# A decoder layer on one core: the hand-written orders of five engines replaced by other ones

## The chip, the core and the metric

One NeuronCore of a Trainium2 chip runs the kernel. TensorE (PE in the profile), VectorE (DVE), ScalarE (ACT), GpSimd (POOL) and SyncE (SP) each run a list of instructions of their own, in order, and meet by semaphores. The metric is the device time of one launch in microseconds; lower is better.

## The reference, cut to what is computed

Eight sequences of 256 tokens with 512 features pass through three sublayers, each with a residual and a layer norm behind it.

```python
x = _layernorm(x + attn(x))           # part A
x = _layernorm(x + xattn(x, ctx))     # part B
x = _layernorm(x + ffn(x))            # part C

# A: sign weights, input rounded to 127 steps; 16 heads, 256 tokens as 2 chunks of 128
qkv = bitlinear(x, qkv_w, qkv_b)
attn = softmax(einsum('blhd,blgd->blhg', q, k) * scale)   # over the heads of one token
out = einsum('blhg,blgd->blhd', attn, v) + einsum('blhd,bhde->blhe', q, kv_state)
return bitlinear(rmsnorm(out, norm_w), proj_w, proj_b)

# B: 32 heads, window of 64 keys of ctx beside 64 keys of x, linear bias by distance
q = concat([ctx, x]) @ Wq;  k, v from x and ctx;  o = softmax(q k / 4 + bias, mask) v;  return o @ Wo

# C: dense layer plus eight low-rank experts, the best two of them weighted
return x @ base_w.T + base_b + 2 * sum_e gate_e * ((x @ A_e) @ B_e)
```

## The kernel before

**Steps and lags.** The batches b = 0 to 7 go through a software pipeline. Each engine has three tables: `first` (its stages up to the loop), a table for one loop step, which is run for i = 2 to 6, and `last`. A row of a table names a stage and the batch it works on. In the loop table the batch is written as a lag: NEXT is batch i+1, A is i, B is i-1, C_ is i-2 and D_ (defined, but used only after the change) is i-3. An engine runs its rows strictly in this order; each stage begins with its waits, so a stage whose input is late holds back all that stands behind it on that engine.

```python
def run(eng, first, stages, last):
    for b, stage in first: stage(b)
    for i in range(2, NB - 1):
        for lag, stage in stages:
            if 0 <= i - lag < NB: stage(i - lag)
    for b, stage in last: stage(b)
```

**Part A**, per batch, on PE: `a1` turns the rounded input (L788), six `a1_qkv` products (L800, each followed by a VectorE pass L1234 that empties the one PSUM bank), `a1_qt` (L809), `a1_state` (L816), two `a1_v` turns (L832; ScalarE copies both results, L610), then per chunk t `a2_s` (L847, L852: head scores), `a2_m` (L861: the turned maxima), `a2_x` (L870, L873: scores again with the maxima taken off; ScalarE's exp is L621) and `a2_v` (L883, L886); `a2_rec` (L891), `a3_t` (L900), two `a3` (L910). The layer norm ends in the ScalarE stage `a4` (L634), which writes x1.

**Part B**: `b1_x1` turns x1 (L921, two halves), `b1_c` turns ctx (L930); `b1_qc` (L946), `b1_kc` (L954), `b1_q` (L963), `b1_k` (L971) and `b1_v` (L981) are the projections. `b2` has eight pieces, b2(half, pair) (L1005 to L1019): scores whose maxima VectorE takes piece by piece (L1352); pair n+1 waits for the maxima of pair n. `b2_max` (L1027) turns them. Then come eight score pieces `b3_s` 0 to 7 (L1040 to L1049), each exponentiated by ScalarE (L700) into p_b; piece m+1 needs the PSUM banks of piece m, so it waits for that exp. `b3_w` 0 to 7 (L1065) are the products with the values. Pieces 3 and 7 are half as long. VectorE turns and divides the result (`b3`, `b3_on`, `b3_of`, L1378 to L1394), `b4` has four pieces (L1074), VectorE adds the residual (`b4_z`, L1399) and takes the layer-norm sums, GpSimd one power (L538), and ScalarE's `b4_x2` (L634) writes x2.

**Part C**: `c1_x2` (L1088), `c1` (L1095: router and low-rank inputs), the choice of two experts on VectorE (`c1`, `c1_top`, L1418 to L1449) with one exp on ScalarE, `c2_gates` (L1103), four half products c2(t, half) (L1113; the second half of each also L1115), and VectorE's `c2_z` (L1457) which adds the part that GpSimd's `c1` (L543) has prepared: x2 plus the base bias. `c2_y` on ScalarE ends it.

**GpSimd** also scales the input and the output of part A (`a0` L509, `a3` L529), forms x plus the projection bias (`a1` L517) and takes the powers of the other norms (L524, L534, L548). **SP** loads x and ctx and stores y, one transfer of 512 KB each per batch.

**Filler.** `keep_on` (L781) puts products of constants into PE's list, in batch 0 and batch 7 alone. They compute nothing that is used. Of batch 7: 4 ahead of each `b3_s`, 12 ahead of the first `b4`.

Of the kernel before, what the change touches and what calls it, by code (L numbers as in the profile page):

```python
# [1545 lines left out]
```

How the kernel before makes its waits and increments, by code:

```python
            def __call__(self, eng, b, k=None):  # L138
                eng.wait_ge(self.sem, self.upto(b, k))
# [1 line left out]
            def before(self, eng, b):  # L141
                if not (isinstance(b, int) and b == 0):
                    eng.wait_ge(self.sem, self.per * b)
# [11 lines left out]
            def link(self, ins):  # L156
                self.k += 1
                ins.then_inc(self.s.sem, 1)
                self.eng.wait_ge(self.s.sem, self.s.per * self.b + self.k)
# [253 lines left out]
            def raw_load(n):  # L413
                if n >= 2:
                    sp.wait_ge(signed.sem, n - 1)
                    sp.wait_ge(summed.sem, n - 1)
                sp.dma_start(raw[n % 2], pieces[n].rearrange("(a p) c -> p a c", p=P)).then_inc(raw_in[n % 2].sem, 16)
# [24 lines left out]
            def late(b):  # L443
# [10 lines left out]
                    loads.append((rl[:, k, E:].rearrange("p (e r) -> p e r", e=E),  # L454
                                  d["L0_ffn_lora_A"][:, k * P:(k + 1) * P, :].rearrange("e p r -> p e r")))
                assert len(loads) == LATE
                for dst, src in loads:
                    sp.dma_start(dst, src).then_inc(late_in.sem, 16)
                sp.wait_ge(turned.sem, 6)
                for n, w in enumerate(("Wsk", "Wk")):
                    sp.dma_start(wk_raw[:, n * KT:(n + 1) * KT, :],
# [32 lines left out]
        @block.gpsimd  # L494
# [3 lines left out]
            pool.wait_ge(zeroed.sem, 2)  # L498
            pool.memset(v_b[:, :, :, DB:DB + 1], 1.0).then_inc(zeroed.sem, 1)
            pool.wait_ge(zeroed.sem, 3)
```

## Time and profile before

| | us |
|---|---|
| median of 3 runs | 990.68 |
| lowest, highest | 988.96, 991.64 |
| the profiled execution, its own time | 988.25 |
| its span in the trace | 986.4 |
| PE busy in that span | 831.1 |
| DVE, ACT, POOL busy | 520.7, 325.1, 85.7 |

The profiled execution took 1.85 us more than its span, which is the time around the first and last instruction. The median stands 2.4 us above it. In the trace a row is a run of like instructions on one engine: its start, the time from its first start to its last end, the engine, the line, the operation, the tiles and the count; what stands in brackets is the idle time just before it and who ended it. A matmul of float32 data shows as two rows' worth (x8 for four). The last matmul of a row overlaps the first of the next, so a stage occupies PE for a little less than its row says.

### The profile page before, as it was taken

To read this page: it belongs to the slowest core of one execution; us is meant where nothing else is said; L and a number is where in the kernel's file an instruction comes from. 1 tells how busy PE (TensorE), PEld (TensorE's weight loads), DVE (VectorE), ACT (ScalarE), POOL (GpSimd) and SP (SyncE) were. 2 spreads that over 40 slices of the span, in tenths; PEclk is the share of its full clock that TensorE was granted. 3 is DMA by queue.
4 is the path that set the end of the run, shared out by engine and by line. 5 is a ranking of instruction groups with operands and counts; after the bars stand their busy time and mean duration, and the time that the engine had idled before them with its cause. 6 is when DMAs were issued, how large, how long until landed. Compare 5 with 4: busy or idle time off the path is not lost.

```text
span 986.4 us, 22679 instructions
## 1 busy us (share of the span) xinstructions
PE 831.1 (84%) x10257; PEld 522.6 (53%) x10257; DVE 520.7 (53%) x1058; ACT 325.1 (33%) x420; POOL 85.7 (9%) x103
## 2 busy tenths in 40 slices
...
DMA packets 18815, 27.08 MB, mean 27 GB/s; under 512 B 5400, under 2 KB 7576, under 8 KB 18720
## 3 DMA queue, kind: packets, MB, share of 16 engines
...
## 4 chain that ended last, share of the span: by engine, by line
PE 60%; ACT 15%; DVE 14%; issue 6%; SPq 2%; DMA 2%; POOL 1%; ACTq 0%; POOLq 0%; DVEq 0%
ACT p_b L700 9%; PE ps L1040 7%; PE ps L1074 6%; PE ps L963 5%; PE ps L1113 5%; DVE max_b L1352 4%; PE ps L946 4%; PE ps L1005 4%; PE ps L981 3%; PE ps L800 2%; SPq L458 2%; PE ps L1049 2%; PE ps L873 2%; PE ps L971 1%; PE ps L852 1%
## 5 line engine op out<-in xcount | busy, mean ns | idle before, releaser
L700 ACT ACTIVATE p_b<-ps 128x2048 f32<-128x2048 f32 x64 | 106.5, 1664 | 102.3 <-PE ps L1049 102.3
L1352 DVE TENSOR_REDUCE max_b<-ps 128x4 f32<-128x768 f32 (+2 forms) x160 | 106.0, 711 | 39.3 <-PE ps L1019 34.1
L1040 PE MATMUL ps<-q_b,k_b 32*128 32x512 f32 (+1 forms) x512 | 66.7, 591 | 26.1 <-ACT p_b L700 23.5
L1005 PE MATMUL ps<-k_b,q_b 32*128 32x192 f32 (+2 forms) x1024 | 56.3, 334 | 21.2 <-DVE max_b L1352 15.7
L1378 DVE STREAM_TRANSPOSE o_nat<-ps 128x512 f32<-128x512 f32 x32 | 21.0, 695 | 96.7 <-PE ps L1065 96.7
L1074 PE MATMUL ps<-wo,o_fb 128*128 128x512 f32 x128 | 62.9, 630 | 4.0 <-DVE o_fb L1394 4.0
L1065 PE MATMUL ps<-p_b,v_b 128*32 128x256 f32 (+1 forms) x1024 | 61.7, 358 | 2.7 <-ACT p_b L700 2.0
L1113 PE MATMUL ps<-base_t,x_t 128*128 128x512 f32 x128 | 62.6, 615 | 1.3 <-DVE x L1457 0.9
L1005 PEld LDWEIGHTS ps<-k_b,q_b 32*128 32x128 f32 x1024 | 39.2, 184 | 45.8 <-DVE max_b L1352 28.4
L946 PE MATMUL ps<-c_t,wq 128*128 128x256 f32 x256 | 61.8, 386 | 1.7 <-DVE nat L1234 0.9
L1252 DVE TENSOR_REDUCE max_a<-ps 128x8 f32<-128x1024 f32 x32 | 37.7, 1220 | 48.2 <-PE ps L852 48.2
L1234 DVE SCALAR_TENSOR_TENSOR nat<-ps,st_a,qkv_bias 128x512 f32<-128x512 f32 x48 | 35.4, 738 | 50.9 <-PE ps L800 50.9
L963 PE MATMUL ps<-x_t,wq 128*128 128x256 f32 x256 | 60.7, 384 | 0.0
L800 PE MATMUL ps<-qkv_sign,xq_t 128*128 128x512 bf16 x192 | 53.9, 406 | 7.9 <-DVE nat L1234 6.8
L781 PE MATMUL ps<-cb 128*128 128x512 bf16 x211 | 54.3, 391 | 6.0 <-DMA rl<-L_ffn_lora_A 3.9
L1270 DVE STREAM_TRANSPOSE sum_a<-ps 128x512 f32<-128x512 f32 x16 | 11.5, 717 | 89.2 <-PE ps L886 76.1
L690 ACT ACTIVATE maxt_b<-ps 128x1024 bf16<-128x1024 bf16 x16 | 16.4, 1023 | 126.8 <-PE ps L1027 126.7
L946 PEld LDWEIGHTS ps<-c_t,wq 128*128 128x128 f32 x256 | 46.4, 190 | 10.9 <-issue 5.5
L963 PEld LDWEIGHTS ps<-x_t,wq 128*128 128x128 f32 x256 | 46.7, 190 | 7.0 <-issue 0.6
L1040 PEld LDWEIGHTS ps<-q_b,k_b 32*128 32x128 f32 x512 | 20.2, 184 | 56.9 <-ACT p_b L700 50.2
L1065 PEld LDWEIGHTS ps<-p_b,v_b 128*32 128x32 f32 x1024 | 26.2, 109 | 27.3 <-issue 11.6
L883 PE MATMUL ps<-p_a,nat 128*32 128x128 f32 x512 | 28.1, 294 | 14.0 <-ACT p_a L621 14.0
...
## 6 DMA issues: line engine op xcount, KB each, us to landing
...
```

Source lines behind the costliest of these rows:

```text
L700: act.activation(p_b[:, j % 2, :, 0:cols], ps[:, 4:8, 0:cols], ACT.Exp, scale=DB ** -0.5).then_inc(pb_here.sem, 1)
L781: pe.matmul(bank(0 if alone else 5), eyeb, bc("sel"), start=True, stop=True)
L800: mm = pe.matmul(bank(0), xq_t[:, k, t * P:(t + 1) * P], qkv_sign[:, k, w * C:(w + 1) * C], start=(k == 0), stop=(k == KT - 1))
L946: mm = pe.matmul(bank(0)[:, (hh % 2) * N:(hh % 2 + 1) * N], wq[:, k, hh, :], c_t[:, k, :], start=(k == 0 and hh % 2 == 0), stop=(k == KT - ...
L963: mm = pe.matmul(bank(4 + n)[:, (hh % 2) * N:(hh % 2 + 1) * N], wq[:, KT + k, hh, :], x1_t[:, k, :], start=(k == 0 and hh % 2 == 0), stop= ...
L1005: pe.matmul(bank(4 + r)[:, (i % 2) * N:(i % 2) * N + 2 * n * S], q_b[strip[r], i, :, :].rearrange("p h q -> p (h q)"), k_b[strip[r], half, ...
L1040: pe.matmul(bank(4 + r)[:, 0:nb * P], k_b[strip[r], half, 2 * j:2 * j + 2, :, :].rearrange("p c s k -> p (c s k)"), q_b[strip[r], 2 * j:2 ...
L1065: mm = pe.matmul(o, v_b[:, j, 4 * half + r, :], p_b[:, j % 2, r, 2 * n * nq:2 * (n + 1) * nq].rearrange("p (h q) -> p h q", h=2), start=(j ...
L1074: mm = pe.matmul(bank(4 + t), o_fb[:, k, t * P:(t + 1) * P], wo[:, k, :], start=(k == 0), stop=(k == G - 1))
L1113: pe.matmul(bank(1), x2_t[:, k, t * P:(t + 1) * P], base_t[:, k, :], start=(k == 0), stop=False)
L1252: dve.tensor_reduce(max_a[:, 0, 2 * n:2 * n + 2, :], ps[:, 2 * n:2 * n + 2, :].rearrange("p a (c n) -> p a c n", c=HT), AX.X, ALU.max).the ...
L1352: ins = dve.tensor_reduce(max_b[:, half, 0, i:i + k, 2 * n:2 * n + 2], ps[:, 4 + 2 * n:6 + 2 * n, :].rearrange("p r (i n) -> p i r n", i=2 ...
```

## The change

The five lists of stages are the same stages with the same instructions; no tile, buffer, transfer size or filler count is altered. Only the three tables of each engine are written in a new order. A few rows cross from one step to the next, which shows as a new lag.

SP and GpSimd in full:

```diff
-            first = [(0, late), (1, a0), (0, b1), (2, a0), (1, b1)]
-            last = [(7, b1), (5, c2), (6, c2), (7, c2)]
-            run(sp, first, [(NEXT, a0), (A, b1), (C_, c2)], last)
+            first = [(0, late), (1, a0), (0, b1), (2, a0)]
+            last = [(6, b1), (7, b1), (4, c2), (5, c2), (6, c2), (7, c2)]
+            run(sp, first, [(B, b1), (NEXT, a0), (D_, c2)], last)
...
-            first = [(0, a0), (0, a1), (0, a3), (1, a0), (0, a4), (1, a1), (1, a3), (2, a0), (2, a1)]
-            last = [(6, a4), (5, b4), (7, a3), (5, c1), (7, a4), (5, c2), (6, b4), (6, c1), (6, c2), (7, b4), (7, c1), (7, c2)]
-            run(pool, first, [(B, a4), (C_, b4), (A, a3), (C_, c1), (NEXT, a0), (NEXT, a1), (C_, c2)], last)
+            first = [(0, a0), (0, a1), (0, a3), (1, a0), (1, a1), (0, a4)]
+            last = [(4, b4), (6, a3), (7, a0), (7, a1), (6, a4), (4, c1), (4, c2), (5, b4), (5, c1), (7, a3), (5, c2), (7, a4), (6, b4), (6, c1),
+                    (6, c2), (7, b4), (7, c1), (7, c2)]
+            run(pool, first, [(D_, b4), (B, a3), (A, a0), (A, a1), (B, a4), (D_, c1), (D_, c2)], last)
```

Of TensorE's loop table the beginning, and the end (the tables of ScalarE and VectorE are rewritten in the same way):

```diff
-            run(pe, first, [(C_, of(b3_s, 0)), (A, of(a1_qkv, 1, [0])), (C_, of(b3_s, 1)), (A, of(a1_qkv, 1, [1])), (C_, of(b3_w, 0)),
...
-                            (NEXT, of(a1_qkv, 0, [2]))], last)
+            run(pe, first, [(A, of(a1_qkv, 1, [0])), (C_, of(b3_s, 3)), (C_, of(b3_w, 2)), (C_, of(b3_s, 4)), (C_, of(b3_w, 3)), (D_, of(c2, 1, 1)),
...
+                            (C_, of(c2, 1, 0)), (B, of(b3_s, 1)), (B, of(b3_w, 0)), (NEXT, of(a1_qkv, 0, [2])), (B, of(b3_s, 2)), (B, of(b3_w, 1))], last)
```

All lines of code behind GpSimd's tables move down by one, so L1040 of before is L1041 of after.

**Place 1: TensorE, the exp pieces of part B in a loop step**, from the end of score piece 0 on. L1049 or L1050 closes a score piece, L1065 or L1066 is a product with values, L800 or L801 one `a1_qkv`, L1114 one half of a `c2`. Before:

```order
L1049 MATMUL ps<-cb 128x8x32 x8
L800 MATMUL ps<-qkv_sign,xq_t 128x512 x4
L1040 MATMUL ps<-q_b,k_b 128x512 x4
L1044 MATMUL ps<-maxt_b,cb 128x512 x4
L1049 MATMUL ps<-cb 128x8x32 x8
L800 MATMUL ps<-qkv_sign,xq_t 128x512 x4
L1065 MATMUL ps<-p_b,v_b 32x2x128 x8
```

After:

```order
L1050 MATMUL ps<-cb 128x8x32 x8
L801 MATMUL ps<-qkv_sign,xq_t 128x512 x4
L1114 MATMUL ps<-base_t,x_t 128x512 x2
L1041 MATMUL ps<-q_b,k_b 128x512 x4
L1045 MATMUL ps<-maxt_b,cb 128x512 x4
L1050 MATMUL ps<-cb 128x8x32 x8
L1066 MATMUL ps<-p_b,v_b 32x2x128 x8
L801 MATMUL ps<-qkv_sign,xq_t 128x512 x4
```

A half of `c2` has moved between score pieces 0 and 1. Further on in the same stretch the second half, c2(1,1), stands between pieces 4 and 5, and the six `a1_qkv` of a batch are spread over the pieces 0 to 7 (one ahead of piece 0, one each behind pieces 0, 1, 2, 5 and 6); before, three of them stood there and half a `b1_qc`.

**Place 2: TensorE, from the last product with values of part B to the first head scores' exp** in a loop step. L946 or L947 is `b1_qc`, L809/L810 `a1_qt`, L816/L817 `a1_state`, L832/L833 `a1_v`, L1074/L1075 `b4`, L847/L848 and L852/L853 `a2_s`, L922 `b1_x1`, L861/L862 `a2_m`. Before:

```order
L946 MATMUL ps<-c_t,wq 128x256 x4
L809 MATMUL ps<-cf,nat 128x128 x4
L816 MATMUL ps<-nat 128x128 x4
L832 MATMUL ps<-cf,sum_a 128x32 x16
L1074 MATMUL ps<-wo,o_fb 128x512 x2
L832 MATMUL ps<-cf,sum_a 128x32 x16
L1074 MATMUL ps<-wo,o_fb 128x512 x2
L847 MATMUL ps<-cb 128x512 x4
L852 MATMUL ps<-k,q 128x128 x16
L1074 MATMUL ps<-wo,o_fb 128x512 x4
L861 MATMUL ps<-cb,maxp_a 128x128
```

After:

```order
L810 MATMUL ps<-cf,nat 128x128 x4
L1075 MATMUL ps<-wo,o_fb 128x512 x2
L817 MATMUL ps<-nat 128x128 x4
L1075 MATMUL ps<-wo,o_fb 128x512 x4
L833 MATMUL ps<-cf,sum_a 128x32 x16
L1075 MATMUL ps<-wo,o_fb 128x512 x2
L833 MATMUL ps<-cf,sum_a 128x32 x16
L848 MATMUL ps<-cb 128x512 x4
L853 MATMUL ps<-k,q 128x128 x16
L922 MATMUL ps<-cf,x 128x128 x4
L862 MATMUL ps<-cb,maxp_a 128x128
L922 MATMUL ps<-cf,x 128x128 x4
```

`b4` now stands around `a1_state` and the first `a1_v`; nothing is left between the second `a1_v` and `a2_s`, and `b1_x1` has moved up to stand right behind `a2_s`. Both pieces of `b1_v` (64 products each) now stand between `a2_x` and `a2_v`, where before there was nothing.

**Place 3: TensorE, the last batch's exp pieces up to its `b4`**, from the last half score piece on (L781/L782 is filler). Before:

```order
L1065 MATMUL ps<-p_b,v_b 32x2x128 x8
L1065 MATMUL ps<-p_b,v_b 32x2x64 x8
L781 MATMUL ps<-cb 128x512 x12
L1074 MATMUL ps<-wo,o_fb 128x512 x8
```

After:

```order
L1066 MATMUL ps<-p_b,v_b 32x2x128 x8
L1114 MATMUL ps<-base_t,x_t 128x512 x2
L1066 MATMUL ps<-p_b,v_b 32x2x64 x8
L1114 MATMUL ps<-base_t,x_t 128x512 x2
L1116 MATMUL ps<-lora_b,gm_t 128x512
L782 MATMUL ps<-cb 128x512 x12
L1075 MATMUL ps<-wo,o_fb 128x512 x8
```

The `c2` of batch 6, which before was over ahead of batch 7's exp pieces, now stands within and behind them; batch 5's last `c2` halves and batch 7's `a3_t` and `a3` have moved in the same way into batch 6's exp pieces.

## Rows read from the trace of the kernel before

**Rows 1.** The page, part 1: busy time of the engines, share, instructions.

```profile
PE 831.1 (84%) x10257; PEld 522.6 (53%) x10257; DVE 520.7 (53%) x1058; ACT 325.1 (33%) x420; POOL 85.7 (9%) x103
```

**Rows 2.** Stretches between score pieces 0: length; PE, PEld, DVE, ACT, POOL busy; clock.

```profile
0.00:180.30 180.30, 128.00 (x1524) 84.47 (x1524) 95.12 (x152) 55.51 (x83) 18.10 (x26) 0.96 0.32 91
180.30:287.10 106.80, 94.59 (x1246) 60.87 (x1245) 62.03 (x129) 36.60 (x47) 9.77 (x11) 0.99 0.02 7
287.10:395.00 107.90, 95.55 (x1245) 61.45 (x1245) 63.59 (x132) 38.00 (x49) 10.44 (x12) 0.98 0.05 16
...
717.20:820.40 103.20, 89.26 (x1220) 58.33 (x1220) 57.22 (x118) 36.31 (x48) 7.00 (x8) 1.00 0.04 12
820.40:915.50 95.10, 81.78 (x875) 47.55 (x874) 34.60 (x84) 25.39 (x28) 4.54 (x5) 0.96 0.02 7
```

**Rows 3.** Timeline of TensorE: exp pieces of one step.

```profile
397.25 1.04 PE L800 MATMUL ps<-qkv_sign,xq_t 128*128 128x512 bf16 x4 [0.67 <-DVE nat L1234]
398.69 1.14 PE L1040 MATMUL ps<-q_b,k_b 32*128 32x512 f32 x8 [0.40 <-ACT p_b L700]
...
404.80 1.07 PE L1065 MATMUL ps<-p_b,v_b 128*32 128x256 f32 x16
...
415.90 1.14 PE L1040 MATMUL ps<-q_b,k_b 32*128 32x512 f32 x8 [1.11 <-ACT p_b L700]
```

**Rows 4.** Timeline of ScalarE, the same step: exp, copy, two norms.

```profile
400.38 1.88 ACT L700 ACTIVATE p_b<-ps 128x2048 f32<-128x2048 f32 x1 [1.75 <-PE ps L1049]
...
430.27 1.08 ACT L610 ACTIVATE nat<-ps 128x512 f32<-128x512 f32 x2 [2.87 <-PE ps L832]
...
440.86 1.52 ACT L634 ACTIVATE x<-x,rs_b 128x512 f32<-128x512 f32 x2
442.47 1.52 ACT L634 ACTIVATE x<-out_a,rs_a 128x512 f32<-128x512 f32 x2
```

**Rows 5.** Timeline of TensorE behind the exp pieces.

```profile
427.50 0.44 PE L832 MATMUL ps<-cf,sum_a 32*128 32x32 f32 x16 [1.24 <-issue]
...
433.28 3.70 PE L1074 MATMUL ps<-wo,o_fb 128*128 128x512 f32 x8
...
441.00 0.65 PE L883 MATMUL ps<-p_a,nat 128*32 128x128 f32 x8 [2.08 <-ACT p_a L621]
...
446.28 0.30 PE L981 MATMUL ps<-wkv,c_t 128*32 128x128 f32 x1 [0.74 <-ACT x_t L654]
```

**Rows 6.** Timeline of VectorE: residual behind b4; two operations of the router.

```profile
437.87 0.67 DVE L1399 TENSOR_TENSOR x<-ps,x 128x512 f32<-128x512 f32 x1
...
473.52 1.10 DVE L1420 TENSOR_TENSOR g_c<-g_c,gs_c 128x16 f32<-128x16 f32 x1
...
475.33 0.17 DVE L1433 TENSOR_TENSOR g_c<-g_c,gs_c 128x16 f32<-128x16 f32 x1
```

**Rows 7.** Timeline of TensorE: pieces of b2 and what stands between them.

```profile
479.92 0.93 PE L1005 MATMUL ps<-k_b,q_b 32*128 32x192 f32 x16 [0.88 <-DVE max_b L1352]
...
488.06 0.93 PE L1005 MATMUL ps<-k_b,q_b 32*128 32x192 f32 x16 [0.62 <-DVE max_b L1352]
...
494.00 1.88 PE L1113 MATMUL ps<-base_t,x_t 128*128 128x512 f32 x4
```

**Rows 8.** Timeline of GpSimd in the same step.

```profile
472.10 2.48 POOL L543 TENSOR_TENSOR x<-x,base_bias 128x512 f32<-128x512 f32 x2
```

**Rows 9.** Timeline of TensorE ahead of the loop, batch 0 and 1.

```profile
103.53 1.11 PE L921 MATMUL ps<-cf,x 128*128 128x128 f32 x4 [1.36 <-ACT x L634]
```

**Rows 10.** Timeline of TensorE in the last batches: filler and b4.

```profile
852.04 9.72 PE L1074 MATMUL ps<-wo,o_fb 128*128 128x512 f32 x16 [3.37 <-DVE o_fb L1394]
...
921.61 1.04 PE L781 MATMUL ps<-cb 128*128 128x512 bf16 x4
...
946.53 0.70 PE L1074 MATMUL ps<-wo,o_fb 128*128 128x512 f32 x1 [0.67 <-DVE o_fb L1394]
```

**Rows 11.** Products of a2_v in two steps: ns of one, min/median/max.

```profile
L883 PE MATMUL ps<-p_a,nat x32: 272/273/297, 226.9 to 228.3; 128*32 128x128 f32 x32
...
L883 PE MATMUL ps<-p_a,nat x32: 419/421/421, 441.0 to 443.8; 128*32 128x128 f32 x32
```

More of the change, by code:

```diff
@@ new lines, in _ @@
+            run(act, first, [(C_, of(b3, 3)), (C_, of(b3, 4)), (C_, of(b3, 5)), (C_, of(b3, 6)), (C_, of(b3, 7)), (B, of(b1_qc, 1)), (A, a1_q),
+                             (D_, c2_y), (B, of(b1_k, 0)), (A, a1_state), (A, a1_v), (C_, of(b4_x2, 0)), (C_, of(b4_x2, 1)), (B, of(a4, 0)),
+                             (B, of(a4, 1)), (A, of(a2_m, 0)), (B, of(b1_x1, 0)), (B, of(b1_x1, 1)), (A, of(a2_x, 0)), (B, b1_v), (B, of(b1_k, 1)),
+                             (A, of(a3_sq, 0)), (A, of(a2_m, 1)), (A, of(b1_c, 0)), (A, of(b1_c, 1)), (A, of(a2_x, 1)), (A, of(a3_sq, 1)),
+                             (C_, of(c1_x2, 0)), (C_, of(c1_x2, 1)), (C_, c1), (A, of(b1_qc, 0)), (B, of(b2, 0)), (A, b1_kc), (A, a3_t), (C_, c2),
+                             (NEXT, a1), (B, of(b2, 1)), (B, of(b3, 0)), (B, of(b3, 1)), (B, of(b3, 2))], last)
@@ L1126, in _ @@
-                     (1, of(a1_qkv, 1, [0])), (0, of(b1_q, 0, range(2))), (1, of(a1_qkv, 1, [1])), (1, of(a1_qkv, 1, [2])),
-                     (0, of(b1_qc, 1, range(2))), (0, of(b1_qc, 1, range(2, KT))), (1, a1_qt), (1, a1_state), (1, of(a1_v, 0)), (0, b1_k),
-                     (1, of(a1_v, 1)), (1, of(a2_s, 0, range(HT))), (0, of(b1_v, range(2))), (0, of(b1_q, 1, range(2))), (1, of(a2_m, 0)),
-                     (1, of(a2_x, 0, range(HT))), (0, of(b1_q, 0, range(2, KT))), (1, of(a2_v, 0)), (0, of(b1_q, 1, range(2, KT))),
@@ L1130, in _ @@
-                     (1, of(a2_s, 1, range(HT))), (0, of(b1_v, range(2, KB))), (1, of(b1_c, 0)), (1, of(a2_m, 1)), (1, of(b1_c, 1)),
-                     (1, of(a2_x, 1, range(HT))), (0, of(b2, 0, 0)), (0, of(b2, 0, 1)), (1, of(a2_v, 1)), (0, of(b2, 0, 2)), (1, a2_rec),
-                     (0, of(b2, 0, 3)), (1, of(b1_qc, 0, range(2))), (1, of(b1_qc, 0, range(2, KT))), (0, of(b2_max, 0)), (0, of(b2, 1, 0)),
-                     (1, b1_kc), (1, a3_t), (0, of(b2, 1, 1)), (1, of(a3, 0)), (0, of(b2, 1, 2)), (1, of(a3, 1)), (2, a1), (0, of(b2, 1, 3)),
@@ new lines, in _ @@
+                     (1, of(a1_qkv, 0, [0])), (1, of(a1_qkv, 0, [1])), (0, of(b1_x1, 0)), (1, of(a1_qkv, 0, [2])), (0, of(b1_x1, 1)),
+                     (1, of(a1_qkv, 1, [0])), (1, of(a1_qkv, 1, [1])), (0, b1_k), (1, of(a1_qkv, 1, [2])), (0, of(b1_qc, 1, range(2))),
+                     (0, of(b1_qc, 1, range(2, KT))), (1, a1_qt), (1, a1_state), (1, of(a1_v, 0)), (0, of(b1_q, 1, range(2))), (1, of(a1_v, 1)),
+                     (1, of(a2_s, 0, range(HT))), (0, of(b1_v, range(2))), (0, of(b1_q, 0, range(2))), (1, of(a2_m, 0)), (1, of(a2_x, 0, range(HT))),
```

215 lines of the change are left out of this document (106 added, 109 removed).

## The prediction

> **What bounds the kernel now.** I read the page first: TensorE is busy 831.1 us of the 986.4 and VectorE 520.7 [rows 1]. Then I cut the span where a batch begins its exp pieces. A loop step takes 106.8 to 107.9 us, and TensorE is busy 94.6 to 95.6 of it, VectorE about 63 [rows 2]; the five steps together take 536.9. So a step is TensorE's list plus some 12 us in which it waits for an answer of another engine, and since no instruction is added or removed, those 12 us are all that a new order can win there. Last I read TensorE's timeline of the step that begins at 395.00, wait by wait, and put under each place what now stands there. The waits fall in three stretches.
>
> **Stretch 1, the exp pieces (place 1).** Score piece at 398.69, its exp from 400.38 for 1.88 [rows 3, 4]: from piece to piece at least 3.6 us, of which the piece itself is about 1.5. That leaves a window of 2.1 us. A product with values fills 1.0 of it (row of 1.07), so with that alone TensorE waits 1.11 [rows 3]. Before, the waits of 0.67, 0.40 and twice 1.11 make 3.3, and smaller ones about 0.5 more. After, piece 0 is followed by one `a1_qkv` (a row of 1.04, 0.9 net) and half a `c2` (1.88 [rows 7]): 2.8, no wait. Pieces 1, 2, 5 and 6 get a product and an `a1_qkv`, 1.9, a wait of 0.2 each; piece 4 gets a short product and 2.8 of `c2`, no wait; the two short pieces leave 0.2 each. Sum 1.2. **Gain 2.6 a step.** The work put in there is taken from elsewhere, where it hid other waits; that is charged in stretch 3.
>
> **Stretch 2, from `a1_qt` to `b1_v` (place 2).** Before: 1.24 ahead of the first `a1_v`, 2.08 ahead of `a2_v` for the exp, 0.74 ahead of `b1_v` [rows 5], and two small ones, together about 4.8. After, `b4` covers the first, 3.7 us of `b1_v` the second, `a2_x` the third. Three waits are new. `a2_s` stands directly behind the second `a1_v` and needs ScalarE's two copies, 1.08 [rows 4] and two handovers: 1.25. `b1_x1` stands directly behind `a2_s` and needs x1: ScalarE writes it behind x2 in its queue, and x2 needs VectorE's norm of `b4` and a GpSimd power. In the trace that chain runs from 437.87 [rows 6] to the first half of the x1 row, 442.47 + 0.76 = 443.23 [rows 4]: 5.4, and 0.1 to start. From the end of `b4` TensorE has the second `a1_v`, the wait of 1.25 and `a2_s` to do, 2.9 together. So it waits 2.5; `a2_m` and all of part A's second half are queued behind. A further 0.3 falls at `a2_m`. Sum 4.05. **Gain 0.7 a step.**
>
> **Stretch 3, the pieces of `b2`.** Before: 0.88 and 0.62 [rows 7] and about 1.2 in smaller ones, 2.7. After: b2(0,1) stands directly behind b2(0,0). The like pair at 488.06 waited 0.62 with a 0.6 us `a1` between, so 1.25. The two `c1_x2` share a bank and have lost the piece between them: one ScalarE copy, 0.75. `b1_kc` waits for a copy that is now behind the router's exp in ScalarE's queue, which waits for VectorE: 0.95. b2(1,1) keeps its 0.62. Ahead of b2(1,2) VectorE now does the third part of the expert choice: 0.9. Small ones 0.5. Sum 5.0. **Loss 2.3 a step.** These sizes are worked out from VectorE's queue and are the least certain; half or one and a half times the new ones would move a step by 1 us.
>
> Steps: 2.6 + 0.7 - 2.3, with the rounding 1.1; **five steps 5.5 us**.
>
> **GpSimd.** While its base-bias sum ran from 472.10 to 474.58 [rows 8], VectorE's small subtraction of two SBUF tiles took 1.10, and it ended with the sum [rows 6]; without company the same operation takes 0.17 to 0.18, as its neighbours do. The wait of 0.88 on TensorE stands behind that queue. The new order puts that sum at the end of the step, behind `a1` and `a4`, beside VectorE passes that read PSUM. So up to 0.9 of VectorE's time per step comes free, already counted in the waits of stretch 3. Added is a wait: `c2_z` needs the sum, and `a1_nat` of the next batch is queued behind `c2_z`. GpSimd ends 0.7 + 2.5 us after the norm sums; VectorE reaches `c2_z` only after the maxima's turn, an `a1_qkv`, its pass and a transpose, 3.5 after them: at most 0.3 late, taken as nothing.
>
> The Trainium skill, page SBUF — State Buffer, section Who interferes with whom, says that a VectorE instruction with two SBUF inputs and a GpSimd instruction that reads SBUF lock each other out, whoever came first. The trace agrees with 1.10 against 0.17. By that rule alone one would credit 0.9 a step, 5 us more; I do not, since it is VectorE's time and not TensorE's.
>
> **Ahead of the loop.** The stretch to batch 0's first piece takes 180.3 [rows 2]. TensorE waits 1.36 for `b1_x1` [rows 9]; now an `a1_qkv` stands in front of it, and GpSimd's `a1` no longer falls on the norm's last step. `a1_qkv` comes 1.5 earlier, and the half clock around 103 and two of the VectorE waits fall away: 2.5. b2(0,0) ahead of `a2_x` hides a maxima wait: 1.2. The rest to piece 0: 1.0. **Gain 4.7**; nothing would be the low bound, for which the reason would be that VectorE's transposes, now between its passes, hold the next `a1_qkv`.
>
> **The last batches (place 3).** From batch 5's piece 0 to batch 6's the time is 103.2, and from there to batch 7's 95.1 [rows 2]. The new order takes 6.9 us of `c2`, `a3_t` and `a3` out of the first and puts them into batch 6's exp windows, and it covers the wait of 3.37 ahead of batch 6's `b4` with half a `c2` and half a `b1_qc`; that `b4` took 9.72 for 16 passes, where 8 take 3.70 in a step, so 2.3 more goes with it [rows 5, 10]. Counted window by window, batch 7's piece 0 comes 8.8 us earlier. Then most is given back: all of batch 6's `c2`, 9.4 us, stands in batch 7's exp windows, which already hold a product (1.07) and four fillers (1.04) [rows 3, 10]. The windows overflow by 0.25, 0.6, 2.05, 0.9 and 1.5, and behind the last product 2.8 of `c2` and twelve fillers (2.8) stand where 3.4 is what `b4` needs: 2.05 more. 7.3 given back. **Gain 1.5**, bounds -2 and +5. From `b4` of batch 7 on the lists are the same but for the order of its four pieces.
>
> Sum without the clock: 5.5 + 4.7 + 1.5 = 11.7.
>
> **The clock.** Behind the same wait of 2.08, `a2_v`'s products took 272 ns in one step and 421 in another [rows 5, 11]: TensorE's clock went from 2.4 to 1.2 GHz. Of the five steps four hold such a fall, and their mean is 107.4 where the first, least touched, has 106.8, and that one begins with the end of a fall; I take 1.4 us for each, 5.6 in all. The new waits of 1.25 and 2.5 lie close together, and stretch 3 has twice the waiting it had. I take seven falls, 9.8: **loss 4.2**. Bounds: nothing new, 0, and the long fall behind 3.37, 2.3 to 3.4 in each of seven steps.
>
> **Forecast.** 11.7 - 4.2 = 7.5 off the span: 978.9, with the 1.85 around it 980.8; the median stands 2.4 above the profiled execution, so **983**. A measurement of this kernel can tell about 0.3%, 3 us, from no change.
>
> **Rivals.**
> 1. *The clock holds*, and the waits at `b1_x1` do not matter to it, as they did not in four of six steps behind 2.08. Then 11.7 or a little more comes through: 979, and to 972 where stretch 3's waits are half as long as I count. Chance 0.18.
> 2. *Given back in stretch 3.* The step gain is a small difference of two sums. If the new waits there are 1 us a step longer, steps come out level, and 4.7 + 1.5 - 4.2 = 2.0 remains: 989. For it: VectorE is busiest there. Chance 0.22.
> 3. *Slower, by the clock.* If the two waits of place 2 bring the fall that 3.37 brought (the long one, 9.72 for `b4`), each of seven steps pays 3 us, 21 against 5.6 now: 11.7 - 15.4 = -3.7, 994. It turns to a loss where a step pays more than 2.5. For it: the sum of both waits is 3.8 with 1.2 us of work between; against: alone, 2.08 often cost nothing. Chance 0.14.
>
> The Trainium skill, page TensorE: Matmul & The Clock Gate, section A second HAM failure mode: psum-queue depth-cycling, says that frequent short idles between groups of matmuls can make the clock swing and pay at each turn. By it rival 3 is the likely one; the trace agrees only in part, with two falls behind six like waits.
>
> The forecast itself: 0.46, its own range 979 to 987. Faster by over 0.3%: 0.46 + 0.18 = 0.64; within 0.3%: 0.22; slower: 0.14. The range 973 to 992 leaves out half of rival 3 and the far end of rival 1.
>
> **What would show it.** A step of about 106.5; waits for the exp ahead of score pieces down from 1.11 to 0.2; no wait of 2.08 at `a2_v`; a new one of about 2.5 at `b1_x1` behind ScalarE's x1 and 1.25 at `a2_s`; the router's subtraction at 0.2; batch 7's `b4` only about 7 us earlier than before although its piece 0 is some 15 earlier. Wrong would be the forecast if `b1_x1` waits little (then faster), if `b2` waits add up to over 6 us, or if most steps show products of `a2_s` to `b1_v` at 421 ns.

## The result, and the profile after

The changed kernel takes **965.73 us** (median of 4 runs, 963.07 to 967.28); beside it on the same chip the kernel before took 990.18 (988.96 to 991.64). The ratio is 0.976, with a 95% interval of 0.9729 to 0.9791. The forecast was 983 with a range of 973 to 992: the direction was right, the size was not, and the time lies 7 us under the low end. The profiled execution has a span of 963.5 against 986.4, 22.9 less.

The page of the changed kernel, its first part (busy time, share, instructions), answers to [rows 1]:

```profile
PE 818.2 (85%) x10209; PEld 527.2 (55%) x10257; DVE 517.7 (54%) x1058; ACT 324.0 (34%) x420; POOL 85.6 (9%) x103
```

The stretches from one score piece 0 to the next, for [rows 2] (length; busy time of PE, PEld, DVE, ACT, POOL with instructions; granted clock; DMA):

```profile
0.00:175.50 175.50, 123.97 (x1508) 83.28 (x1520) 93.31 (x150) 55.76 (x83) 18.16 (x26) 0.97 0.32 93
175.50:277.30 101.80, 88.01 (x1226) 59.87 (x1230) 59.68 (x127) 36.26 (x48) 8.65 (x11) 0.98 0.04 13
277.30:382.30 105.00, 94.39 (x1240) 62.77 (x1244) 63.22 (x132) 37.61 (x50) 10.55 (x13) 0.97 0.06 16
382.30:485.90 103.60, 93.37 (x1240) 61.94 (x1244) 63.13 (x132) 37.57 (x49) 10.48 (x13) 0.98 0.05 18
485.90:590.50 104.60, 94.39 (x1240) 62.74 (x1244) 63.10 (x132) 37.57 (x49) 10.43 (x13) 0.97 0.06 16
590.50:694.10 103.60, 93.36 (x1240) 61.94 (x1244) 63.14 (x132) 37.57 (x49) 10.46 (x13) 0.98 0.04 13
694.10:794.50 100.40, 88.95 (x1207) 59.74 (x1210) 54.51 (x114) 35.55 (x47) 6.36 (x7) 0.97 0.04 12
794.50:883.90 89.40, 76.32 (x867) 45.58 (x874) 35.78 (x78) 26.14 (x28) 5.94 (x7) 1.00 0.02 7
883.90:963.50 79.60, 65.44 (x441) 29.38 (x447) 21.84 (x69) 19.95 (x20) 4.58 (x5) 0.95 0.04 14
```

Read it as three parts. Up to batch 0's pieces: 180.3 before, 175.6 now, 4.7 won. The five loop steps: 536.9 before, 518.6 now, **18.3 won**. From batch 5's pieces to the end: 269.2 before, 269.4 now, nothing. So what was missed lies in the loop, where 5.5 less the clock was forecast. (The stretch ahead of it differs by several us between executions of the same code; more on that below.) The first step is also shorter than the rest and has fewer instructions, 1226 products against 1240 and 127 VectorE instructions against 132: it comes back below. PE lists four products fewer than weight loads (PEld) in a step, 1240 against 1244: their rows are missing from this trace, not from the kernel, and from the traces of all kernels here but the kernel before. Where the first product of a group has no row, the profile shows 0.16 us of idle time that is no wait. In the step that begins at 382.31 this is so at three groups; one of them:

```profile
389.47 0.81 PE L801 MATMUL ps<-qkv_sign,xq_t 128*128 128x512 bf16 x3 [0.16 <-issue]
```

The waits that the prediction named stand in TensorE's timeline of the step that begins at 382.31 (start, us, engine, line, operation, operands, count, and in brackets the idle time before it and who ended it):

```profile
425.38 0.40 PE L848 MATMUL ps<-cb 32*128 32x512 bf16 x4 [1.28 <-ACT nat L611]
425.60 1.07 PE L853 MATMUL ps<-k,q 32*128 32x128 f32 x32
429.35 1.08 PE L922 MATMUL ps<-cf,x 128*128 128x128 f32 x4 [2.69 <-ACT x L635]
430.23 0.31 PE L862 MATMUL ps<-cb,maxp_a 128*128 128x128 bf16 x1
430.34 1.06 PE L922 MATMUL ps<-cf,x 128*128 128x128 f32 x4
...
453.30 0.93 PE L1006 MATMUL ps<-k_b,q_b 32*128 32x192 f32 x16 [1.25 <-DVE max_b L1353]
...
462.27 0.63 PE L1089 MATMUL ps<-cf,x 128*128 128x128 f32 x4 [0.78 <-ACT x_t L705]
...
468.84 1.99 PE L955 MATMUL ps<-c_t,wkv 128*128 128x256 f32 x8 [0.55 <-ACT qc_b L687]
```

Forecast were 1.25 for `a2_s`, 2.5 for `b1_x1`, 1.25 for b2(0,1), 0.75 for `c1_x2`, 0.95 for `b1_kc`. The walk through the new order was good to 0.4 us or better at every place. The four transposes behind the wait of 2.69 take 1.08 instead of 0.66: the clock is at 1.2 GHz there, and it is so in each of the five steps, for 3.4 or for 6.8 us.

The router's subtraction, which GpSimd's sum held for 1.10 us in [rows 6], in VectorE's timeline of the same step, and GpSimd's own timeline, where that sum (L543) now ends the step:

```profile
467.88 0.17 DVE L1421 TENSOR_TENSOR g_c<-g_c,gs_c 128x16 f32<-128x16 f32 x1
```

```profile
484.47 0.70 POOL L534 TENSOR_TENSOR rs_a<-rs_a,cf 128x2 f32<-128x2 f32 x1 [1.47 <-DVE rs_a L1324]
485.14 2.50 POOL L543 TENSOR_TENSOR x<-x,base_bias 128x512 f32<-128x512 f32 x2
```

Three theories for the 13 us that the loop gained beyond the forecast were tried. **V**: GpSimd's sum at its new place frees VectorE, and that is worth more than was counted. **H**: TensorE's own time fell, since its list has fewer breaks and changes of kind; no row shows this as a wait. **K**: the clock cost or gave more than was counted.

### The profile page after: what moved, and what is told of

Its sections match the earlier page's. It is cut to its first block, busy times and chain, and to the rows that moved or that the text cites. A ratio compares the mean times of both kernels' runs of the same rounds, so it can differ in the third digit from the quotient of the medians.

```text
span 963.5 us, 22628 instructions
## 1 busy us (share of the span) xinstructions
PE 818.2 (85%) x10209; PEld 527.2 (55%) x10257; DVE 517.7 (54%) x1058; ACT 324.0 (34%) x420; POOL 85.6 (9%) x103
## 4 chain that ended last, share of the span: by engine, by line
PE 59%; DVE 18%; ACT 12%; issue 5%; SPq 2%; DMA 2%; POOL 1%; ACTq 0%; POOLq 0%; DVEq 0%
ACT p_b L701 8%; DVE max_b L1353 7%; PE ps L1041 7%; PE ps L1075 6%; PE ps L964 6%; PE ps L1114 5%; PE ps L947 4%; PE ps L1006 3%; PE ps L982 3%; PE ps L874 2%; SPq L458 2%; PE ps L1050 2%; PE ps L884 2%; PE ps L801 2%; PE ps L972 2%
## 5 line engine op out<-in xcount | busy, mean ns | idle before, releaser
L1041 PE MATMUL ps<-q_b,k_b 32*128 32x512 f32 (+1 forms) x512 | 66.2, 586 | 14.3 <-ACT p_b L701 8.2
L1114 PE MATMUL ps<-base_t,x_t 128*128 128x512 f32 x128 | 63.9, 625 | 1.8 <-ACT gm_t L714 0.9
L947 PE MATMUL ps<-c_t,wq 128*128 128x256 f32 x256 | 60.9, 385 | 4.1 <-DVE out_a L1276 3.1
L1066 PE MATMUL ps<-p_b,v_b 128*32 128x256 f32 (+1 forms) x1024 | 61.5, 358 | 1.8 <-ACT p_b L701 1.8
L1075 PE MATMUL ps<-wo,o_fb 128*128 128x512 f32 x128 | 58.8, 597 | 0.0
L782 PE MATMUL ps<-cb 128*128 128x512 bf16 x191 | 49.4, 388 | 7.3 <-DMA rl<-L_ffn_lora_A 3.2
L801 PE MATMUL ps<-qkv_sign,xq_t 128*128 128x512 bf16 x172 | 48.1, 400 | 7.8 <-DVE nat L1235 2.9
L947 PEld LDWEIGHTS ps<-c_t,wq 128*128 128x128 f32 x256 | 46.8, 190 | 13.5 <-issue 7.8
L1041 PEld LDWEIGHTS ps<-q_b,k_b 32*128 32x128 f32 x512 | 20.0, 182 | 47.7 <-ACT p_b L701 36.3
L1066 PEld LDWEIGHTS ps<-p_b,v_b 128*32 128x32 f32 x1024 | 26.1, 109 | 25.5 <-issue 10.3
L622 ACT ACTIVATE p_a<-ps 128x2048 f32<-128x2048 f32 x16 | 30.0, 1877 | 24.1 <-PE ps L874 24.1
L1114 PEld LDWEIGHTS ps<-base_t,x_t 128*128 128x128 f32 x128 | 22.8, 194 | 26.1 <-issue 20.0
```

The lines of the kernel that those rows point to most:

```text
L782: pe.matmul(bank(0 if alone else 5), eyeb, bc("sel"), start=True, stop=True)
L801: mm = pe.matmul(bank(0), xq_t[:, k, t * P:(t + 1) * P], qkv_sign[:, k, w * C:(w + 1) * C], start=(k == 0), stop=(k == KT - 1))
L947: mm = pe.matmul(bank(0)[:, (hh % 2) * N:(hh % 2 + 1) * N], wq[:, k, hh, :], c_t[:, k, :], start=(k == 0 and hh % 2 == 0), stop=(k == KT - ...
L1041: pe.matmul(bank(4 + r)[:, 0:nb * P], k_b[strip[r], half, 2 * j:2 * j + 2, :, :].rearrange("p c s k -> p (c s k)"), q_b[strip[r], 2 * j:2 ...
L1066: mm = pe.matmul(o, v_b[:, j, 4 * half + r, :], p_b[:, j % 2, r, 2 * n * nq:2 * (n + 1) * nq].rearrange("p (h q) -> p h q", h=2), start=(j ...
L1075: mm = pe.matmul(bank(4 + t), o_fb[:, k, t * P:(t + 1) * P], wo[:, k, :], start=(k == 0), stop=(k == G - 1))
```

## The experiments

Steps are quoted for each kernel as the time from score piece 0 to score piece 0. Without a fall of the clock they repeat to a few hundredths (in the new order the second step is always 0.15 longer), so they tell more than the medians. The stretch ahead of the loop does not repeat: with the same code in it, it took 180.3, 178.4, 178.1 and 180.3 us in the four profiled executions of the old order, and 175.6, 175.9, 181.4, 178.9 and 177.1 in five of the new one, with more or less time at half the clock.

### GpSimd's sum put back, in the changed kernel

```
-run(pool, first, [(D_, b4), (B, a3), (A, a0), (A, a1), (B, a4), (D_, c1), (D_, c2)], last)
+run(pool, first, [(D_, b4), (B, a3), (D_, c1), (A, a0), (A, a1), (B, a4), (D_, c2)], last)
```

(and the same move for batch 4's `c1` in `last`)

> The changed kernel with one thing undone: GpSimd's base-bias sum goes back to where it stood, behind a3 and ahead of the next batch's a0 and a1. All other orders stay new. Theory V (the move of that sum frees VectorE in stretch 3, and that is where more gain than forecast came from): the router's subtraction is back at 1.1 us, the waits at the pieces of b2 grow by 1 to 3 us a step, the kernel is 6 to 18 us above the changed one. Theory H (the gain beyond the forecast is TensorE's own time, saved at the breaks in its list): the subtraction is slow again, but 0.9 us of VectorE is worth at most 0.3 a step, the kernel is 0 to 3 us above the changed one, 966 to 969. Theory K (the clock) says nothing of it: 0 to 2 us.

Measured: 980.21 us (977.18 to 982.11), 0.9913 of the kernel before (0.9877 to 0.995), **14.5 above the changed kernel**, within V's 6 to 18 and far beyond H's 0 to 3. Undoing one entry of GpSimd's order takes back more than half of the gain, part of it by the clock. But it is not the subtraction that is held, as V had it (L1421 takes 0.18 here). Two small operations ahead of the maxima's turn are, 0.90 and 1.16 us. VectorE's timeline of this kernel, and those two operations in the changed kernel:

```profile
577.31 1.82 DVE L1353 TENSOR_REDUCE max_b<-ps 128x4 f32<-128x768 f32 x2
579.17 0.90 DVE L1365 TENSOR_SCALAR maxq_b<-max_b 128x32 bf16<-128x32 f32 x1
580.10 1.16 DVE L1366 SCALAR_TENSOR_TENSOR max_b<-max_b,maxq_b 128x32 f32<-128x32 f32 x1
581.30 0.24 DVE L1367 CAST maxq_b<-max_b 128x32 bf16<-128x32 f32 x1
```

```profile
571.14 0.24 DVE L1365 TENSOR_SCALAR maxq_b<-max_b 128x32 bf16<-128x32 f32 x1
571.42 0.21 DVE L1366 SCALAR_TENSOR_TENSOR max_b<-max_b,maxq_b 128x32 f32<-128x32 f32 x1
```

GpSimd's sum (two operations of 1.27 us) runs beside them, and TensorE waits for what they feed:

```profile
578.71 2.49 POOL L543 TENSOR_TENSOR x<-x,base_bias 128x512 f32<-128x512 f32 x2
```

```profile
581.93 0.62 PE L1028 MATMUL ps<-cb,maxq_b 128*128 128x128 bf16 x8 [1.46 <-DVE maxq_b L1368]
```

0.90 - 0.24 + 1.16 - 0.21 = 1.61 us of VectorE, and TensorE's list runs 1.60 later from here on. The change of tile order had put a critical turn of the maxima exactly beside GpSimd's old place. The Trainium skill, page SBUF — State Buffer, section Who interferes with whom, gives the rule: a VectorE instruction with two SBUF inputs, or one in a two-port mode, and a GpSimd instruction that reads SBUF take turns as wholes. The rows agree: each of the two held operations ended within 0.1 us of one of the sum's two. That the TENSOR_SCALAR, with one input, was in a two-port mode would fit this, but no row shows the mode. TensorE paid for all of it. Besides, the five steps hold eight falls of the clock instead of five; three of them begin behind this new wait.

### GpSimd's sum late, in the kernel before

```
-run(pool, first, [(B, a4), (C_, b4), (A, a3), (C_, c1), (NEXT, a0), (NEXT, a1), (C_, c2)], last)
+run(pool, first, [(B, a4), (C_, b4), (A, a3), (NEXT, a0), (NEXT, a1), (C_, c1), (C_, c2)], last)
```

> The kernel before with one thing added in the loop: GpSimd's base-bias sum stands behind a0 and a1 of the next batch. Theory V: the router's subtraction takes 0.17 instead of 1.10 us and the wait of 0.88 at b2(1,0) goes, 0.5 to 0.9 us a step, so 3 to 5 us less than the kernel before, 985 to 987. Theory H: the wait of 0.88 shrinks, but c2's gate then waits for the sum in the old order, net nothing, 988 to 991. If it is slower than the kernel before, c2_z waits for the sum and a1_nat behind it.

Measured: 980.12 us (979.62 to 981.95), 0.9911 (0.9878 to 0.9943), 10 us under the kernel before, twice what V expected; H expected no change. The last three of its five steps (the first two take 105.3 as well, without a fall):

```profile
389.00:494.90 105.90, 94.60 (x1240) 61.71 (x1244) 62.55 (x131) 37.95 (x49) 10.40 (x12) 0.98 0.06 16
494.90:600.20 105.30, 93.60 (x1240) 60.64 (x1244) 62.55 (x132) 38.06 (x49) 10.41 (x12) 1.00 0.06 17
600.20:706.30 106.10, 94.79 (x1240) 61.87 (x1244) 62.57 (x132) 37.94 (x50) 10.41 (x12) 0.98 0.05 16
```

The wait of 0.88 ahead of b2(1,0) [rows 7] is gone, and a step without a fall gets shorter by 0.86, from 106.19 (fillers ahead of the exp wait, below) to 105.33. The subtraction itself got shorter by 0.92 (1.10 to 0.17): nearly all of what the sum held on VectorE was time of TensorE. Two falls are left in the loop instead of four; the two that lay around that wait (at 372.6 and 587.6) do not come. With both, the five steps take 528.0 instead of 536.9; 2 more come ahead of the loop, and 3 are lost in the last batches.

### Fillers ahead of the wait for x1, in the changed kernel

```
                     pb_here.before(pe, b)
+                    if 1 <= b < NB - 1:
+                        for _ in range(8):
+                            pe.matmul(bank(7), eyeb, bc("sel"), start=True, stop=True)
```

> The changed kernel with eight filler products, 1.8 us, ahead of the wait of 2.69 us for x1 in batches 1 to 6, so that TensorE works through most of it; nothing waits for them. They tell what the clock's fall in each step costs. Theory K (the fall behind the two waits of place 2 is what a step loses most by, 2 us or more a step): the falls at b1_x1 vanish from the six steps and the kernel is 9 to 14 us below the changed one, 952 to 957. Theory H (a short fall costs 1.4 us at half speed, a long one some 2.4): the falls vanish and the gain is 6 to 10 us, 956 to 960, less what the fillers run over the end of the wait, nothing to 0.2 a step. If the fillers do not hold the clock: 965 to 967.

Measured: **956.99 us** (956.24 to 961.97), 0.9684 (0.9644 to 0.9725), 8.7 under the changed kernel. All five loop steps have a clock of 1.00; the first three:

```profile
181.40:281.90 100.50, 88.28 (x1233) 59.41 (x1238) 59.66 (x127) 36.18 (x47) 8.73 (x11) 1.00 0.04 13
281.90:384.40 102.50, 93.78 (x1247) 61.51 (x1252) 63.06 (x132) 37.46 (x49) 10.46 (x13) 1.00 0.06 16
384.40:486.70 102.30, 93.73 (x1247) 61.46 (x1252) 63.02 (x132) 37.42 (x49) 10.41 (x13) 1.00 0.06 18
```

A step without a fall takes 102.37; with the short one (3.4 us at half speed) 103.60, with the long one (6.8) 104.63. So a fall cost 1.2 or 2.3, and the five steps of the changed kernel lose 518.6 - (100.49 + 4 x 102.37) = 8.6 us to the clock. That is H's row; K's larger price is not there. The median alone, 957.0, lies in the ranges of both. The profiled execution is the slowest of the four (961.97): its loop is 8.4 us shorter than that of the changed kernel, but its stretch ahead of the loop 5.8 longer.

### Fillers ahead of the exp wait, in the kernel before

```
                     keep_on(b, 0, 6)
+                    if t == 0 and b >= 2:
+                        for _ in range(8):
+                            pe.matmul(bank(7), eyeb, bc("sel"), start=True, stop=True)
                     pa_here(pe, b, t + 1)
```

> The kernel before with eight filler products ahead of the wait of 2.08 us for the exp at the first a2_v, in batches 2 to 7. Five falls of the clock lie in its loop, at 1.4 us each by the forecast. Theory K: those falls vanish, 5 to 8 us below the kernel before, 982 to 985. Theory H: likewise up to 5 us, since it prices a short fall the same; the two differ in this only if falls in the kernel before cost more than 1.4. If the falls do not come from this wait, the time stays at 989 to 991.

Measured: 985.28 us (980.86 to 986.62), 0.9955 (0.9938 to 0.9972), at the edge of both expectations. Four of its five steps take 106.17 to 106.22 and hold no fall. That is the number that the prediction lacked: the kernel before without the clock. A fall there cost 0.93 behind the wait of 2.08 (107.13 against 106.19) and 1.7 where it lay among the pieces of `b2` (107.9), and the five steps lost 536.9 - 5 x 106.19 = 5.9 us.

### Both halves of V and K together

The changed kernel with GpSimd's sum back and the eight fillers; and the kernel before with the sum late and its eight fillers (each is two of the edits above).

> The changed kernel with GpSimd's base-bias sum back at its old place and with the eight fillers ahead of x1 in batches 1 to 6. It takes the price of that move apart from the clock. If the two add up: steps of 103.97 us (102.37 with fillers and the sum late, and 1.60 for VectorE's two held operations ahead of b2_max), and most of the difference of 13 us between the two kernels without fillers shrinks to 8 to 9. If the wait ahead of b2_max brings falls of its own in spite of the fillers (three of e1's falls came there): single steps of 104.9 to 105.

> The kernel before with GpSimd's base-bias sum late and eight fillers ahead of the exp wait at the first a2_v in batches 2 to 7: the old order of TensorE with neither the held subtraction nor a fall of the clock. If the parts add up: all steps at 105.33 us, 2.96 over the new order under the same conditions, of which 1.3 is waiting in rows and 1.65 TensorE's time beside its waits. Span 973 to 977.

Measured: 968.37 us (966.69 to 970.05), 0.9769 (0.9713 to 0.9825), and 980.62 (979.08 to 982.15), 0.9892 (0.9838 to 0.9947). The stretches of the first, then of the second:

```profile
279.10:384.70 105.60, 95.33 (x1247) 62.65 (x1252) 64.56 (x132) 37.50 (x50) 10.49 (x12) 0.98 0.06 16
595.50:699.30 103.80, 93.69 (x1247) 61.51 (x1252) 64.54 (x132) 37.49 (x49) 10.48 (x12) 1.00 0.04 13
```

```profile
285.60:390.90 105.30, 95.28 (x1248) 61.33 (x1252) 62.66 (x132) 38.06 (x49) 10.40 (x12) 1.00 0.05 17
390.90:496.30 105.40, 95.28 (x1247) 61.33 (x1252) 62.67 (x132) 38.08 (x50) 10.40 (x12) 1.00 0.05 16
```

The steps of the second are as expected to a hundredth: five of 105.33 or 105.34; its span, 980.3, is not (973 to 977). The first has two steps without a fall: the short first one, 102.10, is 1.61 over its 100.49, and the last, 103.78, is 1.41 over 102.37, where 1.60 was expected. The three between take 105.4 to 105.6: a fall follows the wait ahead of `b2_max`, in spite of the fillers elsewhere. So the sum's old place costs 1.4 to 1.6 by waiting and, in a step with a fall, 1.6 to 1.8 more by the clock. The second kernel's median is no better than without its fillers (980.1): its loop gained 1.3 us, and the stretch ahead of it came out 2 us and the last batches 1 us longer in the profile.

### Dummies of two kinds, in the changed kernel

Eighteen small products more per batch, each ahead of a group that overwrites it, at the same places in both kernels. The full kind, and the kind on 32 rows:

```
+pe.matmul(bank(0)[:, 0:32], eyeb, bc("sel")[:, 0:32], start=True, stop=True)
```

```
+pe.matmul(bank(0)[:, 0:32], eyeb[0:32, :], bc("sel")[0:32, 0:32], start=True, stop=True)
```

> The changed kernel with 18 products more per batch, 144 in all: each takes the whole 128x128 array, has 32 columns, and stands ahead of the first product of a group (a1_qkv, a3, b1_kc, b1_k, b1_q, b4, c2, b1_qc), which overwrites it. It is the partner of the next run, of the same count and place. Both theories: a product of the kind that follows it costs its own pitch, 0.05 to 0.06 us, some of it in waits: 4 to 9 us above the changed kernel, 970 to 975.

> The same 144 products at the same places, each on 32 rows of the array instead of 128, so that TensorE changes between products on part of the array and on all of it. Theory H (every such change costs about 0.2 us into the whole array and 0.1 out of it, which no row shows as a wait): 0.15 to 0.3 us for each, 20 to 40 us above the changed kernel, 985 to 1005. Theory V (the time beyond the forecast is all waits for VectorE, a change of kind costs nothing): as the run before, 970 to 975.

Measured: 972.93 us (970.85 to 975.0), 0.9852 (0.9799 to 0.9905), and 979.41 (976.79 to 983.09), 0.991 (0.9882 to 0.9937); spans 968.7 and 981.0 (for the second that is its slowest execution). V expected 970 to 975 for the second too, H 985 to 1005; it lies between. A change of kind costs, but less than H said: a step with the short fall takes 104.1 with the full dummies and 105.7 with the tiled ones, against 103.6, so 0.03 and 0.12 for one, over all eighteen places. Between two groups on the whole array the price is plain. TensorE's timeline from `a1_qt` to `b4` and `a1_state`, in the changed kernel, with the full dummy, with the tiled one:

```profile
623.04 0.60 PE L810 MATMUL ps<-cf,nat 128*128 128x128 f32 x4
623.47 1.88 PE L1075 MATMUL ps<-wo,o_fb 128*128 128x512 f32 x4
625.19 1.05 PE L817 MATMUL ps<-nat 128*128 128x128 f32 x8
```

```profile
628.47 0.60 PE L811 MATMUL ps<-cf,nat 128*128 128x128 f32 x4
628.91 0.18 PE L1081 MATMUL ps<-cb 128*128 128x32 bf16 x1
628.94 1.96 PE L1083 MATMUL ps<-wo,o_fb 128*128 128x512 f32 x4
630.74 1.05 PE L818 MATMUL ps<-nat 128*128 128x128 f32 x8
```

```profile
635.26 0.60 PE L811 MATMUL ps<-cf,nat 128*128 128x128 f32 x4
635.79 0.18 PE L1081 MATMUL ps<-cb 32*128 32x32 bf16 x1
635.90 1.98 PE L1083 MATMUL ps<-wo,o_fb 128*128 128x512 f32 x4
637.72 1.05 PE L818 MATMUL ps<-nat 128*128 128x128 f32 x8
```

From the first row's start to the last's it is 2.15, 2.27 and 2.46. The dummy itself costs 0.12; going to 32 rows and back costs 0.19 more at this place, and no row shows an idle time for it.

### One more round trip, in the fastest kernel

```
-(A, of(b1_c, 0)), (A, of(b1_c, 1)), (A, of(a2_x, 1, range(HT))), (B, of(b2, 0, 0)),
+(A, of(b1_c, 0)), (A, of(a2_x, 1, range(HT))), (A, of(b1_c, 1)), (B, of(b2, 0, 0)),
```

(and ScalarE's copy of the second half behind `a2_x`'s exp)

> The fastest kernel so far, all of whose steps from batch 2's pieces on take 102.36 to 102.39 us (its first step has 4.5 us less to do), with one thing changed in the loop: the second half of b1_c, four transposes on the whole array, moves from ahead of a2_x, 48 products on parts of it, to behind it, on TensorE and in ScalarE's queue. Work and waits stay; TensorE changes between products on parts and on the whole array once more in each direction. Theory H: one such round trip costs 0.2 us, as the dummies of 32 rows cost 0.22 between products on the whole array against 0.11 of their full twins; each step takes 102.57 to 102.6. Rival (order within TensorE's list costs nothing where no row shows a wait): 102.36 to 102.39.

Measured: 975.97 us (975.96 to 975.99), 0.9862 (0.9819 to 0.9906), **22 above its base of 953.87**. Both theories missed, since "waits stay" was wrong. TensorE's timeline:

```profile
561.58 0.65 PE L937 MATMUL ps<-cf,p_b 128*128 128x128 f32 x4
564.37 0.73 PE L1012 MATMUL ps<-k_b,q_b 32*128 32x64 f32 x16 [2.14 <-ACT c_t L660]
564.89 0.29 PE L1019 MATMUL ps<-cb 3*128 3x64 bf16 x8
564.98 0.27 PE L1024 MATMUL ps<-cb 32*128 32x64 bf16 x8
566.48 1.66 PE L1012 MATMUL ps<-k_b,q_b 32*128 32x192 f32 x16 [1.24 <-DVE max_b L1359]
```

b2(0,0) waits for the copy of the second half, and that copy now stands behind an exp in ScalarE's queue. With that wait the piece at 566.48 comes 2.55 us later in its step than without it, and with the old wait of 1.24 right behind it the clock falls in each of the five steps (that piece takes 1.66 where 0.93 is usual), 1.6 us more in this one. The round trip itself can still be read: the four transposes and `a2_x` begin 0.53 and 1.44 apart, where the same pieces take 0.44 and 1.34 without it, 0.2 in all. It agrees with the dummies, but as a test of the step time this run is spoiled.

### More fillers, and one swap on ScalarE

First: more fillers in batch 7 (ahead of its last three b2 pieces 4, 6, 8, 8 for 4, 4, 2, 2; ahead of `c1_x2` 17 for 14; ahead of `c2_gates` 21 for 15). Then eleven ahead of batch 1's `a1_qkv` pieces. Then the swap:

```
-(C_, c1), (A, of(b1_qc, 0)), (B, of(b2, 0)), (A, b1_kc)
+(A, of(b1_qc, 0)), (C_, c1), (B, of(b2, 0)), (A, b1_kc)
```

> The kernel with eight fillers ahead of x1 in batches 1 to 6, and more of them in the last batch: 16 instead of 8 ahead of its last three b2 pieces, 17 instead of 14 ahead of c1_x2, 21 instead of 15 ahead of c2_gates. The falls of the clock at 872 and 940 should go, worth 1.8 and 1.6 us by the rows of that run. Theory K: 3 to 4 us below it, 953 to 954. If the fillers run past the ends of the waits, 0 to 1 us above it.

> The run before with 11 fillers more, ahead of the a1_qkv pieces of batch 1, which stand in waits of 1.12, 0.85 and 0.85 us beside the half clock at 104 to 111 in the prologue. Theory K: half a fall to one fall less, 0.7 to 2 us below the run before. If the half clock there comes from the waits ahead of a1 instead, which stay: 0 to 1 us above it.

> The fastest kernel so far with one pair swapped in ScalarE's queue in the loop: the copy of b1_qc ahead of the router's exp. It tests the wait of 0.55 at b1_kc, which the forecast put at 0.95 because the copy stands behind an exp that waits for VectorE. If it waits for the exp: the wait falls by 0.3 to 0.5 us a step, and the steps take 101.9 to 102.1, unless the expert choice, now 0.5 later, moves the wait at c2_gates and b2 up by the same, then 102.4. Time 951 to 954.

Measured: 955.49 us (952.59 to 956.71; 953 to 954 was expected), then 953.87 (953.21 to 954.84), then **951.28** (949.18 to 953.58). Against the kernel before the ratios are 0.9671 (0.9636 to 0.9707), 0.9662 (0.9626 to 0.9699) and 0.9621 (0.9586 to 0.9656); their intervals overlap, so the order of the three rests on their traces. The falls at 872 and 940 are gone in the first; in the third the row at `b1_kc` reads

```profile
562.15 1.99 PE L961 MATMUL ps<-c_t,wkv 128*128 128x256 f32 x8 [0.21 <-ACT qc_b L687]
```

0.21 instead of 0.55, and its steps take 102.17 instead of 102.37. Of the 0.34, 0.09 comes back at b2(1,1), which waits 0.85 instead of 0.76; nothing at `c2_gates`.

## Why the prediction was wrong, point by point

The gain of 22.9 taken apart, all from the profiled executions:

| part | forecast | measured | from |
|---|---|---|---|
| ahead of the loop | 4.7 | 4.7 | 180.3 to 175.6 |
| waits of a step | 1.1 x 5 | 2.3 x 5 | 11.9 to 9.6 |
| TensorE's time beside them | 0 | 1.5 x 5 | 94.2 to 92.8 |
| the shorter first step | 0 | 1.9 | 100.49 against 102.37 |
| last batches | 1.5 | 1.2 | 266.6 to 265.4, the falls taken out |
| clock | -4.2 | -4.0 | loop 8.6 against 5.9, last batches 3.9 against 2.6 |

The steps are those without a fall, 106.19 (fillers ahead of the exp wait) and 102.37 (fillers ahead of the wait for x1); the waits are the rows' idle times over 0.1 us, those of the unfilled kernels, and without the 0.16 that stand for missing rows. The falls of the last batches are priced by the same stretches in runs without them: 2.6 for the one at 850 before; 2.2 and 1.7 for those at 740 and 944 after.

What was right: the last batches (8.5 us won up to batch 7's piece 0, 8.1 without the clock, where 8.8 was forecast, and 7.05 given back in its exp windows where 7.3 was); each new wait, to 0.4 or better; and, in the sum, the clock, where seven falls at 1.4 were taken and there are seven at 1.2 to 2.3, against falls of 0.9 to 2.6 before. That the stretch ahead of the loop came out at 4.7 exactly is luck: over the nine profiled executions of the two orders listed above its mean goes from 179.3 to 177.8, 1.5 us, and it differs by up to 6 between executions. What failed is three steps of the arithmetic of the loop.

**The waits of a step were counted too low before and too high after.** For the old order I put 3.8, 4.8 and 2.7, 11.3 in all; without a fall a step of it has 3.9, 5.2 and 2.8, 11.9. In the step that I read, the wait of 0.47 at `b1_x1` did not show because TensorE was at half speed and came late itself; the rest is two waits of 0.1 to 0.15 that were left out. For the new order I put 1.2, 4.05 and 5.0, 10.25 in all; it has 0.9, 4.0 and 4.7, 9.6. Neither sum is off by more than 7%, but the gain is their difference: 2.3 a step instead of 1.1, 6 us in five steps. The expectation of the kernel before with both edits gives the split of a step as 1.3 of waits and 1.65 beside them; it counts the missing rows as waits, and without them the two are 1.5 and 1.5.

**TensorE's own time was taken as constant.** The prediction says that the 12 us of waiting "are all that a new order can win there": between two rows that list no wait the list was treated as free of cost to rearrange. Off waits and falls, a step went from 94.2 to 92.8. One part can be estimated: the timeline has 21 changes from groups on parts of the array to groups on all of it in a step before and 17 after, and if each change there and back costs the 0.19 that was measured at one place, that makes 0.8. For the other 0.7 there is no test. Two things could hold it. The `b1_v` halves together take 3.52 from start to start where apart they took 3.77. And at a wait 0.16 to 0.35 passes beyond the idle time that the row shows and the usual pitch of the products, and a step has 14 waits over 0.1 where it had 19.

**The loop was counted as five full steps.** The first has 14 products fewer (weight loads: 1230 against 1244), and ten of them are two `c2` pieces of a batch that does not exist. They would take 4.5 us; part of that is waiting instead, and 1.9 is left. The same two pieces were charged at the end, in batch 7's exp windows, where 7.05 was indeed given back; their absence in the first step was credited nowhere.

**GpSimd's sum.** The sentence "I do not, since it is VectorE's time and not TensorE's" is refuted. Moved alone in the kernel before, the sum gives 0.86 of its 0.92 to TensorE in each step, and takes two falls of the clock with it, 10 us in all by the medians, 8.9 of them in the loop. The forecast had this 0.88 in its waits, so the sum did not suffer from it, but the price of leaving the sum where it was would have been misjudged: 14.5 us in the new order. V is therefore right that this one edit is large, twice what it expected in the kernel before, and not about the miss: most of what the sum gives was already counted.

**The rivals.** The one in which the clock holds named the right side for a wrong reason: the clock did not hold. The one in which stretch 3 gives all back did not come: its waits were 4.7, not 6. Of the one that is slower by the clock the mechanism came, a fall in each step behind the two waits of place 2, but its size stayed under the turning point of 2.5 a step: 1.2 or 2.3. The Trainium skill's page TensorE: Matmul & The Clock Gate, section A second HAM failure mode: psum-queue depth-cycling, says that frequent short idles between groups of matmuls can make the clock swing and cost throughput at each turn. The trace of the changed kernel agrees: one fall in each step, at 1.2 or 2.3 us, and fillers in 1.9 of the 2.7 us take it away.
